# Block-sparse and window attention with a gated MLP: the window attention's outputs packed to 128 rows, and its small splits moved to GpSimd

## The reference, cut to what matters

```python
attn = jax.nn.softmax(jnp.einsum('bnhd,bnwhd->bnhw', q, k) * scale, axis=-1)
y_win = jnp.einsum('bnhw,bnwhd->bnhd', attn, v).reshape(Bx, Nq, C)
y_win = _lin(y_win, pj_w[2], pj_b[2])
qn = _ln(Q, n1_w, n1_b)
g = jax.nn.softmax(_lin(qn, g_w, g_b), axis=-1)
y = g[..., 0:1] * y_cmp + g[..., 1:2] * y_sel + g[..., 2:3] * y_win + Q
ym = y.reshape(Bx, Hx, Wx, C)
t = _lin(ym, pin_w)
t = lax.conv_general_dilated(t, dw_w, (1, 1), 'SAME', dimension_numbers=('NHWC', 'HWIO', 'NHWC'), feature_group_count=2 * HID)
x1, x2 = jnp.split(t, 2, axis=-1)
mlp = _lin(jax.nn.gelu(x1, approximate=False) * x2, pout_w)
ym = _ln(ym + mlp, n2_w, n2_b)
```

## Time and profile before

| what | value |
|---|---|
| time, median of 3 runs | 811.15 us (810.43 to 815.52) |
| time of the profiled execution | 802.85 us |
| its span, first to last instruction | 800.7 us |
| PE matmuls busy | 719.6 us, 90% |
| DVE busy | 620.4 us, 77% |
| ACT busy | 374.9 us, 47% |
| POOL busy | 175.0 us, 22% |
| share of the ending chain on PE | 68% |
| share of the ending chain on DVE | 15% |
| share of the ending chain on DMA | 4%, nearly all `RB<-SB` |

### The profile page before, as it was taken

The page is one execution under the profiler, slowest core; times in us unless marked ns, Lnnn a source line. Parts: engine busy times, 40 slices in busy tenths (PEclk is TensorE's granted clock), DMA queues, the critical chain, the costliest instruction groups (busy, mean ns, idle before and its releaser), DMA issues.

```text
span 800.7 us, 19201 instructions
## 1 busy us (share of the span) xinstructions
PE 719.6 (90%) x7639; PEld 457.5 (57%) x7639; DVE 620.4 (77%) x1051; ACT 374.9 (47%) x826; POOL 175.0 (22%) x184
## 2 busy tenths in 40 slices
PE   4989999999999798988888888888889999999994
PEld 2557466666666566666666666656534545455552
DVE  6984888888888467777767787777469889999842
ACT  2077566555543134444444444434434062647564
POOL 2150355555544150000000000001310437300000
PEclk9999999999999668999999999999899999999998
DMA  5000245544469936776767777751100000000001
GB/s 233 0 1 2 70 125 150 140 130 130 137 135 168 162 108 131 139 142 131 142 135 138 137 137 140 142 105 41 28 1 1 0 1 0 0 21 29 32 20 60
DMA packets 79646, 70.97 MB, mean 89 GB/s; under 512 B 10522, under 2 KB 78147, under 8 KB 79046
## 3 DMA queue, kind: packets, MB, share of 16 engines
q1 hardware_dynamic: 61078, 47.51, 25.0%
q10 hardware_dynamic: 18480, 22.24, 14.7%
HBM read 47.46 MB, written 21.57 MB: 86 GB/s over the span
## 4 chain that ended last, share of the span: by engine, by line
PE 68%; DVE 15%; ACT 5%; issue 4%; DMA 4%; SPq 2%; ACTq 1%; DVEq 0%
PE banks L849 13%; DVE wn L1310 6%; PE banks L783 6%; PE banks L675 5%; PE banks L697 5%; PE banks L749 5%; PE banks L562 5%; PE banks L768 4%; PE banks L649 4%; PE banks L799 3%; DMA RB<-SB 3%; PE banks L711 2%; DVE AC L1109 2%; PE banks L676 2%; DVE ON L1328 2%
## 5 line engine op out<-in xcount | busy, mean ns | idle before, releaser
L1310 DVE TENSOR_REDUCE wn<-banks 112x2 f32<-112x560 f32 x224 | 162.3, 737 | 45.0 <-PE banks L749 44.0
L984 ACT ACTIVATE P<-banks 98x448 f32<-98x448 f32 x224 | 119.9, 541 | 154.3 <-PE banks L768 126.6
L849 PE MATMUL banks<-FP,PTB 128*128 128x392 f32 x384 | 129.4, 493 | 1.0 <-DVE c L1341 0.9
L1109 DVE SCALAR_TENSOR_TENSOR AC<-XT,vec,AC 128x1540 f32<-128x1540 f32 (+5 forms) x48 | 115.1, 2401 | 1.1
L849 PEld LDWEIGHTS banks<-FP,PTB 128*128 128x128 f32 x384 | 72.8, 190 | 55.5 <-DVE c L1341 1.6
L783 PE MATMUL banks<-P,Vw 84*17 84x56 f32 (+1 forms) x3584 | 92.1, 221 | 3.0 <-issue 1.7
L749 PE MATMUL banks<-K,Q 126*112 126x280 bf16 x288 | 66.9, 316 | 3.5 <-DVE wn L1310 3.0
L480 POOL TENSOR_TENSOR pk<-pr,pk 128x434 bf16<-128x434 f32 (+1 forms) x42 | 42.8, 1020 | 94.0 <-ACT pk L941 94.0
L783 PEld LDWEIGHTS banks<-P,Vw 84*17 84x17 f32 (+1 forms) x3584 | 54.2, 99 | 15.0 <-issue 5.0
L768 PE MATMUL banks<-Q,K 128*128 128x56 bf16 x1152 | 55.4, 189 | 2.8 <-ACT P L984 1.4
L520 POOL MEMSET FP<- 128x224 f32 x1 | 0.3, 284 | 255.2 <-PE banks L768 255.2
(11 more groups left out here) (231 smaller groups left out, 1187.0 us busy)
## 6 DMA issues: line engine op xcount, KB each, us to landing
k_parts<-pk SPq DMA_DIRECT2D x28, 325.5 KB, 3.9
K<-k_parts ACTq DMA_DIRECT2D x21, 434.0 KB, 5.2
Vw<-v_rows SPq DMA_DIRECT2D x112, 52.1 KB
FP<-k_parts ACTq DMA_DIRECT2D x12, 434.0 KB, 5.2
Vw<-v_rows SPq DMA_DIRECT2D x112, 44.6 KB
q_parts<-pk SPq DMA_DIRECT2D x14, 336.0 KB, 2.5
Q<-q_parts ACTq DMA_DIRECT2D x42, 112.0 KB, 5.5
v_rows<-vst SPq DMA_DIRECT2D x14, 263.5 KB
```

Of the source, the lines that this page charges most:

```text
L849: last = mm(bank(2 + place_in_unit, C, ZPIX), WT[:, dy, part, C * grp:C * (grp + 1)], D[:, part, QROWS * q + dy:QROWS * (q + 1) + dy, :].r ...
L984: a(P[q % 4][0:HKEYS[half], :], PS[0:HKEYS[half], 4 + q % 2, 0:HEADS * SUB], ACT.Exp).then_inc(sem("w_exp"), 1)
L1109: return ve.scalar_tensor_tensor(out=o, in0=src(ro + dy, rn, co + dx, cn), scalar=v(wcol + t), in1=o, op0=ALU.mult, op1=ALU.add)
L1310: ve.tensor_reduce(wn[tl % 2][:, 2 * hp:2 * hp + 2], src, AX.X, ALU.max, negate=True).then_inc(sem("w_slot_read"), 1)
```

## The change

In words:

- **Packing.** After the three `RB` transfers, SP issues four more, one a quadrant: rows of `OB`'s part u = 1 go to the 16 free rows of part u = 0. All 128 rows of `OB[:, 0]` then hold outputs. The sums' rows, which lie in the free rows, have been collected before.
- **D** is one matmul in place of two, and DVE's multiplication covers 392 columns in place of 784. It moves from step 0 to step 2, and waits, on PE and on DVE, for all seven transfers.
- **Y** is one matmul in place of two (each is two passes in fp32), and moves from step 3 to step 4. The projection's bias, once a row of the matrix, is added with the block attention's output (L1275, now with a scalar), and taken off there for the other attentions by a third row of `pjrow`.
- **Splits to POOL.** The maxima's split and five of the six instructions of the reciprocals go from DVE to POOL, at steps 3 mod 4 and 10. POOL's forming of `WT` is spread behind the splits from step 27 on, one instruction each; the memset of `D`'s border and the first three of the MLP's even and odd sums stand in POOL's order before the last job's reciprocals.
- **S** stands behind the scores and the products of its step on PE, no longer between A and the scores.
- PE's first bands of the MLP's projection move with D and Y by one step.

The diff, cut:

```diff
+        RECIPS = 16 * (3 + 4)
...
-            if q % STEPJ == 0:
-                jobs.append(("D", (q - 32) // STEPJ, JOBS))
-            if q % STEPJ == 3:
-                jobs.append(("Y", (q - 35) // STEPJ, JOBS))
+            if q % STEPJ == 2:
+                jobs.append(("D", (q - 34) // STEPJ, JOBS))
+            if q % STEPJ == 4:
+                jobs.append(("Y", (q - 36) // STEPJ, JOBS))
...
-                        sp.dma_start(RB[j % 2][4 * part:4 * part + 4, :, :], SB[j % 2][:, part, :]).then_inc(sem(f"w_recips{j % 2}"), 16)
+                        sp.dma_start(RB[j % 2][HEADS * part:HEADS * (part + 1), :], SB[j % 2][:, part, :]).then_inc(sem(f"w_recips{j % 2}"), 16)
+                    for b in range(4):
+                        sp.dma_start(OB[j % 2][QUAD * b + DH:QUAD * (b + 1), 0, :], OB[j % 2][QUAD * b:QUAD * b + DH, 1, :]).then_inc(sem(f"w_recips{j % 2}"), 16)
...
+            def reciprocal_parts(j):
...
+                pool.wait_ge(sem("w_recip"), j + 1)
...
+                g.tensor_tensor(sr[:], sr[:], SRG[:, img, t, :], ALU.mult).then_inc(sem("w_part"), 1)
+                pool.wait_ge(sem("w_part"), 4 * j + 1)
+                g.tensor_copy(parts[:, 0, :], sr[:]).then_inc(sem("w_part"), 1)
...
+            def split_maxima(tl):
...
+                g.tensor_copy(wnb[tl % 2][:, 0, :], wn[tl % 2][:]).then_inc(sem("w_high"), 1)
+                pool.wait_ge(sem("w_high"), tl + 1)
+                g.tensor_tensor(wnb[tl % 2][:, 1, :], wn[tl % 2][:], wnb[tl % 2][:, 0, :], ALU.subtract).then_inc(sem("w_split"), 1)
...
+            for q in STEP_RANGE:
+                tl = (q + LEAD - 3) // 4
+                if q % 4 == 3 and 0 <= tl < STEPS // 4:
+                    split_maxima(tl)
+                    if q >= 24:
+                        next(taps_todo, None)
+                j = (q - 26) // STEPJ
+                if q % STEPJ == 10 and 0 <= j < JOBS:
+                    reciprocal_parts(j)
+                if q == STEPS - 5:
...
+                    for n in range(3):
+                        even_odd(n)
...
                     if kind == "D":
-                        pe.wait_ge(sem(f"w_recips{n % 2}"), 48 * (n // 2 + 1))
+                        pe.wait_ge(sem(f"w_recips{n % 2}"), RECIPS * (n // 2 + 1))
                         slot_free(order)
-                        for u in range(2):
-                            last = mm(PS[:, 2 * slot + u, 0:BAND], spread[:], RB[n % 2][:, u, :], start=True, stop=True)
-                        last.then_inc(sem("w_slot"), 1)
+                        mm(PS[:, 2 * slot, 0:BAND], spread[:], RB[n % 2][:], start=True, stop=True).then_inc(sem("w_slot"), 1)
                     if kind == "Y":
                         pe.wait_ge(sem("w_norm"), n + 1)
                         slot_free(order)
-                        for u in range(2):
-                            last = mm(PS[:, 2 * slot, 0:BAND], w("pj2", C, C * u), ON[:, u, :], start=(u == 0), stop=(u == 1))
-                        last.then_inc(sem("w_slot"), 1)
+                        mm(PS[:, 2 * slot, 0:BAND], w("pj2"), ON[:], start=True, stop=True).then_inc(sem("w_slot"), 1)
...
-                        dve.wait_ge(sem("w_out"), SUBS * (n + 1))
-                        ve.tensor_tensor(ON[:], OB[n % 2][:], PS[:, 2 * slot:2 * slot + 2, 0:BAND], ALU.mult).then_inc(sem("w_norm"), 1)
+                        dve.wait_ge(sem(f"w_recips{n % 2}"), RECIPS * (n // 2 + 1))
+                        ve.tensor_tensor(ON[:], OB[n % 2][:, 0, :], PS[:, 2 * slot, 0:BAND], ALU.mult).then_inc(sem("w_norm"), 1)
```

More of the change, by code:

```diff
@@ L96, in shape_constants @@
     c[:, CIO] = np.arange(128)
-    for b in range(4):
-        for part in range(3):
-            c[4 * part + b, CD + QUAD * b:CD + QUAD * (b + 1)] = 1
+    for part in range(3):
+        for b in range(4):
+            for u in range(2):
+                at0 = CD + QUAD * b + DH * u
+                c[HEADS * part + 2 * b + u, at0:at0 + DH] = 1
     for n in range(2):
@@ L242, in build @@
             SB = [sb(f"SB{n}", [HEADS * SUBS, 3, SUB], BF16, s3) for n in range(2)]
-            RB = [sb(f"RB{n}", [128, 2, BAND], BF16, s3) for n in range(2)]
-            ON = sb("ON", [128, 2, BAND], F32, s3)
+            RB = [sb(f"RB{n}", [128, BAND], BF16, s3) for n in range(2)]
+            ON = sb("ON", [128, BAND], F32, s3)
         early.close()
@@ new lines, in tap_weights @@
+            def tap_weights():
+                pool.wait_ge(sem("taps_loaded"), 16)
+                pool.wait_ge(sem("c_added"), NGRP)
+                pin2 = bc(w("pin", HID, HID).unsqueeze(1), [128, 3, HID])
+                g.tensor_scalar(half_pin, w("pin", HID, HID), 0.5, None, ALU.mult).then_inc(sem("wt_steps"), 1)
+                g.tensor_tensor(WT[:, :, 0, :], TP[:, :, 0, :], pin2, ALU.mult).then_inc(sem("wt_steps"), 1)
+                yield
+                g.tensor_tensor(WT[:, :, 3, :], TP[:, :, 2, :], pin2, ALU.mult).then_inc(sem("wt_steps"), 1)
+                yield
+                pool.wait_ge(sem("wt_steps"), 3)
+                g.tensor_tensor(TP[:, :, 0, :], TP[:, :, 0, :], TP[:, :, 2, :], ALU.add).then_inc(sem("wt_steps"), 1)
+                yield
+                pool.wait_ge(sem("wt_steps"), 4)
+                g.tensor_tensor(WT[:, :, 1, :], TP[:, :, 0, :], TP[:, :, 1, :], ALU.add).then_inc(sem("wt_steps"), 1)
+                yield
+                g.tensor_tensor(WT[:, :, 2, :], TP[:, :, 0, :], TP[:, :, 1, :], ALU.subtract).then_inc(sem("wt_steps"), 1)
+                pool.wait_ge(sem("wt_steps"), 6)
+                for part in (1, 2):
+                    yield
+                    g.tensor_tensor(WT[:, :, part, :], WT[:, :, part, :], bc(half_pin.unsqueeze(1), [128, 3, HID]), ALU.mult).then_inc(sem("wt_ready"), 1)
@@ L522, in _, with even_odd @@
+            def even_odd(n):
                 m, q = divmod(n, QUARTERS)
@@ L631, in fold_values @@
                         mm(o, VMs[:, m, :], w("pj1"), start=False, stop=False)
-                    last = mm(o, pjrow[0:2, C + KC * j:C + KC * (j + 1)], pjrow[0:2, 0:C], start=False, stop=True)
+                    last = mm(o, pjrow[:, C + KC * j:C + KC * (j + 1)], pjrow[:, 0:C], start=False, stop=True)
                 last.then_inc(sem("p_vp"), 1)
@@ L1274, in _ @@
                     xs = XT[:, img, t * BAND:(t + 1) * BAND]
-                    ve.tensor_tensor(xs, PS[:, 4, 0:BAND], xs, ALU.add).then_inc(sem("c_added"), 1)
+                    ve.scalar_tensor_tensor(out=xs, in0=PS[:, 4, 0:BAND], scalar=v(V_PB2), in1=xs, op0=ALU.add, op1=ALU.add).then_inc(sem("c_added"), 1)
                 if p == PSTEPS + 2:
@@ L1459 @@
     share[0, 0:SC0] = share[1, SC0:] = 1 / HEADS
+    share[2] = -1 / HEADS
     pjb = np.concatenate([a["pj_b"], share], 1)
```

83 lines of the change are left out of this document (33 added, 50 removed).

## The result

The changed kernel took 819.16 us (median of 16 runs, 815.07 to 825.82), the kernel before, beside it, 812.25 us (16 runs). The ratio is 1.014, 95% interval 1.011 to 1.017: slower by 1.4%, some 11 us. I had predicted 797.5 us, faster, with a range of 784 to 815: wrong in sign, and outside the range.

A forecast was written before the change was run, and what follows sets the result against it. PE bounds the kernel before, SP's queue the changed one. Start -3.5, eleven jobs -8.4 and the last two -1.6 give -13.5 us: 789.3 for the profiled execution, 797.5 us from the median 811.15, range 784 to 815.

The forecast's parts named there:

- The bound: In the repeated attention job, SP's queue takes PE's place: 19.8 us of SP a job against PE's 17.4.
- the packing's issue: In SP's queue, each of four added issues a job takes 0.44 us with its gap, bounds 0.28 and 0.76.
- the landing: Ahead of D, the last packing lands in 4.2 us, as `RB` did in 4.42.
- the low clock: Behind D's waits, longer waits can lower PE's clock; 0.8 us a job left for it, making 20.6 us.
- the gain at Y: At Y, two passes of four take 0.8 us; with the delayed step behind, 1.15 in place of 1.91 us.
- rival 3: Slower: packings issue at 0.76 us, SP needs 21.0 us, low clock behind each D; job 22.3, 817 us, chance 0.15.
- The chain from S to D: SP's chain from S at step 9 to the last packing's landing takes 10.2 us; PE needs 9.3 for those steps.
- The wait at D: PE waits at D about 2.4 us a job with SP full, 1 us with SP on time.
- The start: Before the repeated jobs, -3.5 us: no cast collision and its low clock, no early splits, less D standing two steps later.
- The sum: Whole kernel against the profiled execution of 802.85 us: start -3.5, eleven jobs -8.4, last two jobs -1.6, together -13.5 us.
- rival 1: SP's queue isn't felt, or packings cost 0.28: a job 18.4 to 19.3 us, about 778.5 us, chance 0.08.

The follow-up runs named there:

- The fillers: Changed kernel with ten extra, useless matmuls of 448 columns by TensorE ahead of each wait at D but the last two: 807.35 us, ratio 0.9945.

## Why the prediction was wrong, point by point

**The bound** was named half rightly. SP is nearly full, 21.7 us in a 23.4 us job, and the wait came up at D, at the row I named. But SP rests 1.7 us a job: the job isn't as long as SP's issues, as my sum had it, but as long as the chain from S over SP and the landing to D, and what TensorE does at a low clock behind it. Three terms failed: the packing's issue, the landing, and the low clock, which took the gain at Y. I had rival 3 (817 us, chance 0.15) for what happened.

**The packing's issue** is the first mis-sized term: 0.44 us with its gap, against 0.73 + 0.04 measured, so 18.0 + 4 x 0.77 = 21.1 us for SP (21.7 measured, the `RB` and value issues being longer too) and not 19.8. I took the plain two-dimensional issues as nearest, for the shape; the collecting of the sums out of the same tile, 586 ns, was nearest by kind, and the packing's median is 589. The upper bound, 0.76, was the value. (A band is 8 x 56 = 448 pixels and not 392, and a packing's row 1,792 bytes and not 1,568: the rows say 128x448 and 28 KB.)

**The chain from S to D** is the second. Measured from S at 429.11: turn and copy 0.57 us (I had 0.4), maxima 0.76 (0.76), values 1.63 (1.6), `RB` 2.12 (1.95), three packings 1.88 (1.3), landing 6.02 (4.2): 13.0 us in place of 10.2. Two thirds of the error is the landing. I took it from `RB`'s row as if a landing were a constant; it goes with the load, from 1.91 us with the DMA engines busy 0.14 of the time to 5.88 at 0.77, and before it was read at 0.65 (403 to 408 us), without the packings' bytes.

**The wait at D**: 2.4 us predicted, 2.8 measured. Nearly right, but by luck: I let it fill a job of 19.8 us, and it came from a chain 2.8 us longer than mine, in a job of 23.2. PE took 442.14 - 429.11 - 2.27 = 10.8 us for the nine steps, not 9.3; it waited twice for ACT's exponentials there, 0.97 us in all, at the full clock.

**The clock**: 0.8 us a job. The fillers gave back 1.3 a job. I had written that a low clock behind most D would show the gain gone; it lies behind nearly every D.

**Y** shows where that time goes. I gave it 0.8 us for two passes in place of four. The views by line, 300 to 592 us, give a pass in ns (min/median/max), before and changed; the third row is a Y of the kernel with fillers:

```profile
L799 PE MATMUL banks<-ON,W x56: 539/539/1116, 329.0 to 591.2; 128*128 128x448 f32 x56
```

```profile
L850 PE MATMUL banks<-ON,W x24: 539/954/1117, 327.1 to 582.5; 128*128 128x448 f32 x24
```

```profile
438.34 1.02 PE L853 MATMUL banks<-ON,W 128*128 128x448 f32 x2
```

Y now stands just behind D's wait, and in ten of the twelve jobs its two passes took 1.66 to 1.86 us, as long as the four did before (1.77). Where the clock was full they took 1.02.

**What the change gains** elsewhere was right: S step 1.28 us (1.29), `ON` 0.62 (0.6), no wait of PE for GpSimd, no low clock from 295 to 305 us (1.00 there now). The half with splits and turns is worth 1.3%. The start gained 1.1 us, not 3.5; why the rest was lost before the first `ON` wasn't looked into by a run.

**The sum** went from -13.5 to about +11 us. By the runs, of the 25 us 19 are the packings: my forecast stood 19 us above rival 1 (-13.5 against -33), the measured kernel stands 38 above the one without packings, about half of it the wait for them at D with its low clock, the other half their issues on SP and their load on the DMA engines. The other 6 are in the rest, -27 us without packings (-3.3%) where rival 1 had -33.

## What to carry to other kernels

Price a new small transfer by the issue row of the nearest transfer on the same queue and tile, and its landing by how busy the DMA engines are while it lands, its own bytes added. When a queue is 85% full (18.0 of 21.4 us), four more issues can be paid twice, at the transfer that is waited for and at those behind it. Here three other places in the same queue only moved the wait, and another queue took it away. And a wait of two or three microseconds on TensorE costs more than itself in this kernel, since the low clock behind it takes another 1.3 us a job: a few idle matmuls in front of it are a cheap test of how much.

The quickest versions run here are the changed kernel with its packings issued by GpSimd (0.984), the same with fillers (0.985) or with `RB` too (0.986), and the splits and turns alone (0.987). All beat both kernels; their intervals overlap, so which is best is open, and whether packing gains anything over the last of them too.

## What was not expected of the hardware

- The same 28 KB packing landed 1.91, 2.85 and 5.88 us after its issue began, with the DMA engines busy 0.14, 0.20 and 0.77 of the time; 7 KB issued last took as long as 28 KB issued last (5.26 to 6.24 us, but for one of 8.11, against 5.25 to 6.58).
- Packings issued by SP took 574 ns at least and up to 1,670; issued by GpSimd 484 to 712. The collecting of the sums took up to 6.6 us to land.
- Fillers of 1.2 us a job cost nothing in one kernel, within the 0.8% that its ratio is known to: the fuller clock, 0.94 in place of 0.88, and shorter waits gave them back.
